# Second scan of a Mamba-like layer: one pair of states from matmuls with diagonals of B back to GpSimd, and three or four pairs times C there

## The chip, the cores and the metric

The kernel runs on one core of one Trainium2 chip. It is one launch, and the metric is the device time of that launch in microseconds (us). Engines are named TensorE (PE; its weight loads PEld), VectorE (DVE), ScalarE (ACT), GpSimd (POOL) and SyncE (SP, whose queue issues most DMAs).

## The reference, cut to what matters

A gated layer of two halves. The first is a selective state-space layer over four sequences of 1024 positions with 1024 channels and 16 states; the second is a feed-forward block with attention for 128 chosen rows of each sequence. The part touched here is the scan of the first half:

```python
delta = jax.nn.softplus(jnp.einsum('er,brl->bel', dt_proj_w, dt_lo) + dt_proj_b[None, :, None])
A = -jnp.exp(A_log)

def step(state, xs):
    d_t, B_t, C_t, u_t = xs
    dA = jnp.exp(d_t[..., None] * A)
    state = state * dA + (d_t * u_t)[..., None] * B_t[:, None, :]
    y_t = jnp.einsum('ben,bn->be', state, C_t)
    return (state, y_t)
...
y = y + D[None, :, None] * u
y = y * jax.nn.silu(z)
```

## The kernel before

**Stages.** `project_stage` (the first two sequences), `scan_stage` with `first` = 0, `choose_and_attend`, `scan_stage` with `first` = 2 (the second scan, sequences 2 and 3), `choose_and_attend` again with what is left of the feed-forward block. Each stage begins when the one ahead of it is done on all engines. The second scan carries feed-forward matmuls of the first two sequences beside it (`fill`); the first scan carries projections of the last two (`early`).

**Units and chunks.** A scan is 32 units, each one tile of 128 channels by 512 positions. Eight units (all 1024 channels) are a chunk; a sequence has two chunks, so a scan has chunks 0 to 3. In chunks 1 and 3 (called odd; `s // NE % H2` is 1) the scans start from a carry that the chunk ahead left. The 16 states of a unit are handled as 8 pairs, 0 to 7.

**One pair.** ScalarE makes dA = exp(delta A) of its two states. delta u B, the added term, comes from one of three places: GpSimd's product (`quad`, the most common, a whole instruction for the states of a group of four that are its own), matmuls with diagonals of B on TensorE (pairs in `SCALED`), or TensorE's transposes of a term that ScalarE scaled in transposed form (pairs in `TURNED`). In the first case dA goes to the PSUM tile `pA` and the term lies in `x`; in the other two the term goes to `pA` and dA to `x`. `pA` has room for two pairs, the even and the odd ones taking turns, so a pair begins when the one two ahead is out of the way. VectorE scans each state (one instruction of 128x512). Then comes the product with C: on GpSimd for the pairs in `pool_pairs` (the scan then writes to `hp` in SBUF, three buffers), on VectorE for the others (the scan writes in place in `pA`). Both write to `x`. `add_pair` sums the pair into `py` with 8 transposing matmuls; after all eight pairs `gate` on VectorE multiplies by the gate, and GpSimd adds the input (`add_x`).

**What sets the order.** Each engine has one queue, written out by hand in loops over units and pairs, and waits on semaphores in it. On GpSimd a unit s runs: product with C of pair 7 of unit s-1; `quad(s, 2)`, `quad(s, 3)`; C of pair 1; a feed-forward merge in some units; `begin(s + 1)`, which makes the next delta and delta u; C of pair 3; `add_x(s - 1)`; `quad(s + 1, 0)`; C of pair 5; `quad(s + 1, 1)`; C of pair 6. On TensorE: `make_b(1)`, sum of pair 5 of the unit ahead, sum of 6, `make_b(3)`, sum of 7, gate and skip transposes, sum of 0, `make_b(5)`, sum of 1, transposes of the next delta u, sums of 2 and 3, `make_b(7)`, sum of 4, with feed-forward matmuls (`beside`) in between. `make_b(i)` waits for pair i-2: for its product if VectorE makes that, for its scan if GpSimd does. `quad` waits until the sum of the unit ahead has read the part of `x` that it writes. On VectorE a unit is scan of the first state, product with C of the pair ahead (if it is VectorE's), scan of the second state, for pairs 0 to 7; `gate` of the unit ahead stands before pair 3, and two small feed-forward operations stand in some units.

Before the change both scans have `TURNED` = (3, 7) and `SCALED` = (1, 5). `make_diagonals` on GpSimd writes the diagonals of B once a chunk for each scaled pair, two selects each.

Of the kernel before, what the change touches and what calls it, by code (L numbers as in the profile page):

```python
# [25 lines left out]
NE = DI // P  # L26
# [5 lines left out]
H2 = L // HALF  # L32
# [6 lines left out]
SPAN = 2  # L39
# [35 lines left out]
        self.ropes = ctx.enter_context(nc.sbuf_tensor(f"c{first}_ropes", [P, SPAN, 2 * DH], F32))  # L75


TURNED, SCALED = (3, 7), {0: (1, 5), SPAN: (1, 5)}


def states_by_pool(first):
# [287 lines left out]


def pool_pairs(first, s):
    return (1, 3, 5, 6, 7) if s // NE % H2 else (1, 3, 5, 7)


def vec_pairs(first, s):
    return tuple(i for i in range(NPAIR) if i not in pool_pairs(first, s))
# [37 lines left out]
def scan_stage(nc, t, ctx, keep, first, late_taps=None):  # L414
# [14 lines left out]
    scaled = SCALED[first]  # L429
    from_pe = tuple(sorted(TURNED + scaled))  # L430
    NF, ND_B = 2 * len(from_pe), 2 * len(scaled)
    pool_order = [(s, i) for s in range(UNITS) for i in pool_pairs(first, s)]
    vec_order = [(s, i) for s in range(UNITS) for i in vec_pairs(first, s)]
    pool_count = {at: k + 1 for k, at in enumerate(pool_order)}
# [73 lines left out]
    def chunk(s):  # L508
        return s // NE
# [22 lines left out]
    def b_at(s, n):  # L532
        return NF * s + 2 * from_pe.index(n // 2) + n % 2 + 1

    def column(n):
        return 2 * (n // 4) + n % 2
# [15 lines left out]
    with nc.Block() as block:  # L552
# [161 lines left out]
        def _(pool):  # L714
            def begin(s):
                pool.wait_ge(soft_ready, s + 1)
                pool.tensor_tensor(out=delta[:, s % 2], in0=delta[:, s % 2], in1=du[:, s % 2], op=ALU.add).then_inc(delta_ready, 1)
                pool.wait_ge(delta_ready, s + 1)
                if s >= 2:
                    pool.wait_ge(u_in[s % 2], 16 * (s // 2))  # L720
                pool.tensor_tensor(out=du[:, s % 2], in0=delta[:, s % 2], in1=u[:, s % 2], op=ALU.mult).then_inc(du_ready, 1)

            def quad(s, g):
                if s >= UNITS:
                    return
                if g == 0:
                    pool.wait_ge(du_ready, s + 1)
                if s and s % NE == 0:
                    pool.wait_ge(B_in[g], 16 * chunk(s))
                into, n = quad_place(first, g)  # L730
                if s:
                    pool.wait_ge(summed, after_sum(s - 1, (4 * g + n - 1) // 2))
                pool.tensor_tensor(out=x[:, 4 * g:4 * g + n], in0=du[:, s % 2:s % 2 + 1].broadcast_to([P, n, HALF]),  # L733
                                   in1=bB[:, into:into + n], op=ALU.mult).then_inc(w_ready, 1)
# [6 lines left out]
            def make_diagonals(c, i):  # L741
                for n in (2 * i, 2 * i + 1):
                    k = 2 * scaled.index(i) + n % 2
                    if c:
                        pool.wait_ge(BT_in[c % 2], 16 * (NS // 2) * ((c + 1) // 2))
                        pool.wait_ge(b_ready, b_at(c * NE - 1, n))
                    pool.affine_select(out=diagB[:, k], in_=BT[:, c % 2, column(n)].rearrange("p (a o) -> p a o", o=1).broadcast_to([P, HALF // P, P]),
                                       compare_op=ALU.is_equal, fill=0.0, base=0, pattern=[[0, HALF // P], [-1, P]],
                                       channel_multiplier=1).then_inc(diag_ready, 1)

            def times_C(s, i):
                if i not in pool_pairs(first, s):
                    return
                pool.wait_ge(scanned, NS * s + 2 * i + 2)
                if s and s % NE == 0:
                    pool.wait_ge(C_in[i // 2], 16 * chunk(s))
                pool.tensor_tensor(out=x[:, 2 * i:2 * i + 2], in0=hp_of(s, i), in1=bC[:, 2 * i:2 * i + 2],  # L757
                                   op=ALU.mult).then_inc(pool_hc, 1)
# [3 lines left out]
            def add_x(s):  # L762
                pool.wait_ge(y_used, s + 1)
                pool.wait_ge(xt_in[s % 3], ring3(s)[1])
                pool.tensor_tensor(out=xt[:, s % 3], in0=xt[:, s % 3], in1=gy[:, s % 3], op=ALU.add).then_inc(x2_ready, 1)

            def merge(begin, end):
                for p in range(NI // 2):
                    if begin <= up_slot[p] + MERGE_LAG < end:
                        pool.wait_ge(swish_ready, p + 1)  # L770
                        pool.wait_ge(up_ready, p + 1)
                        both = hidden[:, 2 * p:2 * p + 2].rearrange("p m r -> p (m r)")
                        pool.tensor_tensor(out=both, in0=both, in1=swish[:], op=ALU.mult).then_inc(hidden_ready, 1)

            def root(begin, end):
                if begin <= POW_AT < end:
                    pool.wait_ge(mean_ready, 1)
                    pool.wait_ge(exponent, 1)
                    pool.tensor_tensor(out=squares[:], in0=squares[:], in1=minus_half[:], op=ALU.pow).then_inc(pow_ready, 1)
# [8 lines left out]
            for s in range(UNITS):  # L788
                last_tile = s % NE == NE - 1 and s + 1 < UNITS
                if s:  # L790
                    times_C(s - 1, 7)
                quad(s, 2)
                quad(s, 3)
                times_C(s, 1)
                if fill:
                    merge(NPAIR * s, NPAIR * s + NPAIR // 2)
                if s + 1 < UNITS:
                    begin(s + 1)
                if last_tile and scaled:
                    make_diagonals(chunk(s) + 1, scaled[0])  # L800
                if fill:
                    root(NPAIR * s, NPAIR * s + NPAIR // 2)
                times_C(s, 3)
                if s:
                    add_x(s - 1)
                quad(s + 1, 0)
                times_C(s, 5)
                if last_tile and scaled:
                    make_diagonals(chunk(s) + 1, scaled[1])
                quad(s + 1, 1)  # L810
                if fill:
                    merge(NPAIR * s + NPAIR // 2, NPAIR * (s + 1))
                    root(NPAIR * s + NPAIR // 2, NPAIR * (s + 1))
                times_C(s, 6)
# [1582 lines left out]
```

## Time and profile before

| | us |
|---|---|
| median of 3 runs | 2808.98 |
| lowest and highest | 2807.94, 2814.0 |
| profiled execution, its own time | 2810.57 |
| its span | 2808.7 |
| second scan, first scan instruction to last gate, by the trace | 1248.0 to 2110.6 |

The span is the time from the first to the last record of the one profiled execution; its own time holds the launch as well. Busy times of an engine are sums over that span. PE's shares need care: matmuls are pipelined, a diagonal matmul is recorded twice, and the printed duration of one is longer than the distance to the next. Where an engine's cadence is meant, starts are compared.

### The profile page before, as it was taken

What the parts mean: (1) busy time and instruction counts of PE and PEld (TensorE: products, weight loads), DVE (VectorE), ACT (ScalarE), POOL (GpSimd) and SP (SyncE); (2) the same over time, 40 slices, a digit from 0 to 9 for tenths busy, and PEclk for the clock granted to TensorE, in tenths of its full rate; (3) what the DMA queues carried; (4) which work ended last, traced back from release to release, by engine and by line L of the source; (5) the groups of instructions that cost most, each with busy time, mean ns of one, the idle gap of its engine ahead of it and who ended that gap; (6) DMA issues with size and microseconds to landing.
All of it is one profiled execution on the core that took longest, in us unless ns stands there. A gap on an engine that the chain in (4) does not pass through costs nothing. (4 is left out here: it accounts for less than half of the span.)

```text
span 2808.7 us, 38267 instructions
## 1 busy us (share of the span) xinstructions
PE 2534.9 (90%) x13528; PEld 1853.5 (66%) x13528; DVE 1964.8 (70%) x2500; ACT 1616.4 (58%) x3482; POOL 1616.2 (58%) x898
## 2 busy tenths in 40 slices
PE   8979999989999657879999999999997799999998
PEld 3356666666666426556688988888673576578853
DVE  5679999989999786569998988999896544110000
ACT  4578888778887442277787787887661215210000
POOL 1269999999999610028899998889881100000000
PEclk9979999999999858999999999999998899999999
DMA  7732242442332397863344344244228741344442
GB/s 277 260 87 83 64 144 80 127 115 64 116 92 80 110 405 263 291 192 99 121 135 129 103 153 146 84 167 146 85 76 311 273 151 38 97 158 150 152 155 97
DMA packets 252622, 412.53 MB, mean 147 GB/s; under 512 B 50832, under 2 KB 134800, under 8 KB 249872
## 3 DMA queue, kind: packets, MB, share of 16 engines
q1 hardware_dynamic: 238928, 353.98, 39.4%
q10 hardware_dynamic: 12160, 51.39, 4.6%
q0 software_dynamic: 1344, 4.72, 0.5%
q8 instruction: 108, 1.77, 0.3%
q14 instruction: 82, 0.67, 0.1%
HBM read 325.09 MB, written 84.94 MB: 146 GB/s over the span
## 5 line engine op out<-in xcount | busy, mean ns | idle before, releaser
L757 POOL TENSOR_TENSOR s_x<-s_hp,k_bC 128x1024 f32<-128x1024 f32 x288 | 680.2, 2368 | 68.2 <-DVE s_hp L1290 67.7
L733 POOL TENSOR_TENSOR s_x<-s_du,k_bB 128x1024 f32<-128x1024 f32 x254 | 601.5, 2377 | 39.2 <-PE s_py L882 23.6
L882 PE MATMUL s_py<-k_ident,s_x 128*128 128x128 f32 x4096 | 522.2, 274 | 21.4 <-POOL s_x L757 21.4
L882 PEld LDWEIGHTS s_py<-k_ident,s_x 128*128 128x128 f32 x4096 | 463.8, 142 | 32.6 <-POOL s_x L757 28.5
L1214 ACT ACTIVATE s_pA<-s_delta,k_negA 128x512 f32<-128x512 f32 x512 | 333.6, 681 | 190.6 <-DVE s_x L1267 185.1
L1983 PE MATMUL l_p<-l_hT,l_ring 128*128 128x256 f32 x1792 | 389.4, 380 | 2.0 <-ACT l_hT L2088 1.0
L1983 PEld LDWEIGHTS l_p<-l_hT,l_ring 128*128 128x128 f32 x1792 | 341.6, 191 | 49.6 <-issue 1.5
L1290 DVE TENSOR_TENSOR_SCAN s_hp<-s_x,s_carry,s_pA 128x512 f32<-128x512 f32 x256 | 321.7, 1267 | 44.5 <-PE s_pA L864 36.1
L1214 ACT ACTIVATE s_x<-s_delta,k_negA 128x512 f32<-128x512 f32 x512 | 340.6, 710 | 0.0
L1290 DVE TENSOR_TENSOR_SCAN s_hp<-s_x,s_pA 128x512 f32<-128x512 f32 x256 | 310.0, 1211 | 42.3 <-ACT s_x L1214 26.5
L1092 ACT ACTIVATE s_xT<-s_duT,k_BT 128x128 f32<-128x128 f32 x1024 | 336.4, 389 | 0.1
L864 PEld LDWEIGHTS s_pA<-k_bB,s_duT 128*128 128x128 f32 x2048 | 251.0, 196 | 86.2 <-DVE s_hp L1290 68.0
L1290 DVE TENSOR_TENSOR_SCAN s_pA<-s_pA,s_x 128x512 f32<-128x512 f32 x256 | 299.8, 1214 | 4.4 <-ACT s_pA L1214 4.0
L864 PE MATMUL s_pA<-k_bB,s_duT 128*128 128x128 f32 x2048 | 262.8, 283 | 23.0 <-DVE s_hp L1290 23.0
L1267 DVE TENSOR_TENSOR s_x<-s_pA,k_bC 128x1024 f32<-128x1024 f32 x224 | 268.7, 1199 | 17.7 <-DMA k_bC<-scratch_xd 17.7
L1290 DVE TENSOR_TENSOR_SCAN s_pA<-s_pA,s_carry,s_x 128x512 f32<-128x512 f32 x192 | 234.6, 1268 | 1.0 <-ACT s_pA L1214 0.8
L1960 POOL DMA_INDIRECT out_dram<-c_rows,l_row_i x2 | 1.9, 953 | 330.8 <-DVE c_rows L2309 330.8
L862 PEld LDWEIGHTS s_pA<-k_ident,s_xT 128*128 128x128 f32 x1024 | 116.5, 142 | 97.4 <-DVE s_hp L1290 72.1
L862 PE MATMUL s_pA<-k_ident,s_xT 128*128 128x128 f32 x1024 | 135.9, 276 | 39.1 <-DVE s_hp L1290 39.1
L2304 DVE TENSOR_TENSOR t_hidden<-l_silu,l_p 128x256 f32<-128x256 f32 x32 | 13.5, 421 | 208.0 <-PE l_p L1983 208.0
L1990 PE MATMUL l_p<-l_ring,t_hidden 128*128 128x512 f32 x352 | 151.4, 592 | 0.0
L1950 POOL TENSOR_TENSOR l_squares<-l_squares,l_minus_half 128x1 f32<-128x1 f32 x2 | 1.1, 555 | 250.3 <-DVE l_squares L2280 250.3
(238 smaller groups left out, 3770.4 us busy)
## 6 DMA issues: line engine op xcount, KB each, us to landing
k_bC<-scratch_xd SPq DMA_DIRECT2D x32, 1024.0 KB, 11.0
scratch_ug<-p_ug ACTq DMA_DIRECT2D x16, 1024.0 KB, 4.1
k_u<-scratch_ug SPq DMA_DIRECT2D x64, 256.0 KB, 3.5
k_bB<-scratch_xd SPq DMA_DIRECT2D x32, 512.0 KB, 8.3
s_gy<-scratch_ug SPq DMA_DIRECT2D x64, 256.0 KB, 4.5
s_xt<-in_x SPq DMA_DIRECT2D x64, 256.0 KB, 4.8
scratch_x<-s_xt SPq DMA_DIRECT2D x64, 256.0 KB, 3.6
r_x<-scratch_x SPq DMA_DIRECT2D x32, 512.0 KB, 10.2
```

The lines of the kernel that those rows point to most:

```text
L733: pool.tensor_tensor(out=x[:, 4 * g:4 * g + n], in0=du[:, s % 2:s % 2 + 1].broadcast_to([P, n, HALF]), in1=bB[:, into:into + n], op=ALU.mu ...
L757: pool.tensor_tensor(out=x[:, 2 * i:2 * i + 2], in0=hp_of(s, i), in1=bC[:, 2 * i:2 * i + 2], op=ALU.mult).then_inc(pool_hc, 1)
L862: last = nc.tensor.transpose(out, xT[:, k, a * P:(a + 1) * P], ident[:])
L864: last = nc.tensor.matmul(out, duT[:, a * P:(a + 1) * P], diagB[:, 2 * scaled.index(i) + n % 2, a], start=True, stop=True)
L882: last = nc.tensor.matmul(py[:, a], x[:, n, a * P:(a + 1) * P], ident[:], is_transpose=True, start=False, stop=n == NS - 1 and a == HALF / ...
L1092: last = nc.scalar.activation(xT[:, k, a * P:(a + 1) * P], duT[:, a * P:(a + 1) * P], ACT.Copy, scale=BT[:, chunk(s) % 2, column(2 * TURNE ...
L1214: nc.scalar.activation(out, delta[:, s % 2], ACT.Exp, scale=negA[:, s % NE, n:n + 1]).then_inc(dA_ready, 1)
L1267: nc.vector.tensor_tensor(x[:, 2 * i:2 * i + 2], pA[:, j:j + 2], bC[:, 2 * i:2 * i + 2], ALU.mult).then_inc(vec_hc, 1)
L1290: nc.vector.tensor_tensor_scan(out, dA, added, initial, ALU.mult, ALU.add).then_inc(scanned, 1)
L1983: last = nc.tensor.matmul(out[:, 0:ROWS], w[:, c * P:(c + 1) * P], src[:, c], start=c == 0, stop=c == KT - 1)
L1990: last = nc.tensor.matmul(banks[2 * a + h][:], src[:, a * P:(a + 1) * P], w[:, h * HALF:(h + 1) * HALF], start=is_first, stop=is_last)
L2304: nc.vector.tensor_tensor(hidden[:, m], silu[:, m % 2], acc[2 + m % 2][:, 0:ROWS], ALU.mult).then_inc(act_ready, 1)
```

## The change

`SCALED` of the second scan is (5,) instead of (1, 5). So pair 1's term is GpSimd's again: `states_by_pool` has ten states instead of eight, and the first group of four is whole, which makes `quad(s, 0)` one instruction of 128x2048 where it was 128x1024. Pair 1's dA goes to `pA` instead of `x`. `make_b(s, 1)` and pair 1's diagonals are gone. `quad(s + 1, 0)` now waits for the sum of pair 1 where it waited for that of pair 0. `pool_pairs` of the second scan's odd chunks is (1, 5, 7) instead of (1, 3, 5, 6, 7); the even chunks keep (1, 3, 5, 7). So VectorE multiplies pairs 3 and 6 by C in the odd chunks. The first scan stays as it was.

```diff
-TURNED, SCALED = (3, 7), {0: (1, 5), SPAN: (1, 5)}
+TURNED, SCALED = (3, 7), {0: (1, 5), SPAN: (5,)}
...
 def pool_pairs(first, s):
+    if first:
+        return (1, 5, 7) if s // NE % H2 else (1, 3, 5, 7)
     return (1, 3, 5, 6, 7) if s // NE % H2 else (1, 3, 5, 7)
...
-                if last_tile and scaled:
-                    make_diagonals(chunk(s) + 1, scaled[0])
+                if last_tile and 1 in scaled:
+                    make_diagonals(chunk(s) + 1, 1)
...
-                if last_tile and scaled:
-                    make_diagonals(chunk(s) + 1, scaled[1])
+                if last_tile and 5 in scaled:
+                    make_diagonals(chunk(s) + 1, 5)
```

GpSimd, second scan, a unit of chunk 0, from the delta of the next unit on (L717, L721: delta and delta u; L757: product with C; L765: the input; L733: product with B). Before:

```order
L717 TENSOR_TENSOR s_delta<-s_delta,s_du 128x512
L721 TENSOR_TENSOR s_du<-s_delta,k_u 128x512
L757 TENSOR_TENSOR s_x<-s_hp,k_bC 128x1024
L765 TENSOR_TENSOR s_xt<-s_xt,s_gy 128x512
L733 TENSOR_TENSOR s_x<-s_du,k_bB 128x1024
L757 TENSOR_TENSOR s_x<-s_hp,k_bC 128x1024
L733 TENSOR_TENSOR s_x<-s_du,k_bB 128x1024
L757 TENSOR_TENSOR s_x<-s_hp,k_bC 128x1024
L733 TENSOR_TENSOR s_x<-s_du,k_bB 128x1024 x2
L757 TENSOR_TENSOR s_x<-s_hp,k_bC 128x1024
```

The same place now (lines are two further down in the changed file):

```order
L719 TENSOR_TENSOR s_delta<-s_delta,s_du 128x512
L723 TENSOR_TENSOR s_du<-s_delta,k_u 128x512
L759 TENSOR_TENSOR s_x<-s_hp,k_bC 128x1024
L767 TENSOR_TENSOR s_xt<-s_xt,s_gy 128x512
L735 TENSOR_TENSOR s_x<-s_du,k_bB 128x2048
L759 TENSOR_TENSOR s_x<-s_hp,k_bC 128x1024
L735 TENSOR_TENSOR s_x<-s_du,k_bB 128x1024
L759 TENSOR_TENSOR s_x<-s_hp,k_bC 128x1024
L735 TENSOR_TENSOR s_x<-s_du,k_bB 128x1024 x2
L759 TENSOR_TENSOR s_x<-s_hp,k_bC 128x1024
```

Nothing moved; the first product with B is twice as wide. The same stretch of a unit of chunk 1 (with the merge, L773) before:

```order
L717 TENSOR_TENSOR s_delta<-s_delta,s_du 128x512
L721 TENSOR_TENSOR s_du<-s_delta,k_u 128x512
L757 TENSOR_TENSOR s_x<-s_hp,k_bC 128x1024
L765 TENSOR_TENSOR s_xt<-s_xt,s_gy 128x512
L733 TENSOR_TENSOR s_x<-s_du,k_bB 128x1024
L757 TENSOR_TENSOR s_x<-s_hp,k_bC 128x1024
L733 TENSOR_TENSOR s_x<-s_du,k_bB 128x1024
L773 TENSOR_TENSOR t_hidden<-t_hidden,s_swish 128x512
L757 TENSOR_TENSOR s_x<-s_hp,k_bC 128x1024 x2
L733 TENSOR_TENSOR s_x<-s_du,k_bB 128x1024 x2
L757 TENSOR_TENSOR s_x<-s_hp,k_bC 128x1024
```

and now:

```order
L719 TENSOR_TENSOR s_delta<-s_delta,s_du 128x512
L723 TENSOR_TENSOR s_du<-s_delta,k_u 128x512
L767 TENSOR_TENSOR s_xt<-s_xt,s_gy 128x512
L735 TENSOR_TENSOR s_x<-s_du,k_bB 128x2048
L759 TENSOR_TENSOR s_x<-s_hp,k_bC 128x1024
L735 TENSOR_TENSOR s_x<-s_du,k_bB 128x1024
L775 TENSOR_TENSOR t_hidden<-t_hidden,s_swish 128x512
L759 TENSOR_TENSOR s_x<-s_hp,k_bC 128x1024
L735 TENSOR_TENSOR s_x<-s_du,k_bB 128x1024 x2
L759 TENSOR_TENSOR s_x<-s_hp,k_bC 128x1024
```

The products with C of pairs 3 (ahead of L765) and 6 (one of the two behind the merge) are gone. VectorE, a unit of chunk 1, from gate on (the scans are printed as SCALAR_TENSOR_TENSOR at L1290; L1267 is the product with C), before:

```order
L1256 TENSOR_TENSOR s_gy<-s_py,s_gy 128x512
L1290 SCALAR_TENSOR_TENSOR s_hp<-s_x,s_carry,s_pA 128x512
L1267 TENSOR_TENSOR s_x<-s_pA,k_bC 128x1024
L1290 SCALAR_TENSOR_TENSOR s_hp<-s_x,s_carry,s_pA 128x512
L1290 SCALAR_TENSOR_TENSOR s_pA<-s_pA,s_carry,s_x 128x512 x2
L1290 SCALAR_TENSOR_TENSOR s_hp<-s_x,s_carry,s_pA 128x512
L1267 TENSOR_TENSOR s_x<-s_pA,k_bC 128x1024
```

and now:

```order
L1258 TENSOR_TENSOR s_gy<-s_py,s_gy 128x512
L1292 SCALAR_TENSOR_TENSOR s_pA<-s_x,s_carry,s_pA 128x512
L1269 TENSOR_TENSOR s_x<-s_pA,k_bC 128x1024
L1292 SCALAR_TENSOR_TENSOR s_pA<-s_x,s_carry,s_pA 128x512
L1292 SCALAR_TENSOR_TENSOR s_pA<-s_pA,s_carry,s_x 128x512
L1269 TENSOR_TENSOR s_x<-s_pA,k_bC 128x1024
L1292 SCALAR_TENSOR_TENSOR s_pA<-s_pA,s_carry,s_x 128x512
L1292 SCALAR_TENSOR_TENSOR s_hp<-s_x,s_carry,s_pA 128x512
L1269 TENSOR_TENSOR s_x<-s_pA,k_bC 128x1024
```

Pair 3's scans write to `pA`, and its product with C stands between the two scans of pair 4.

## Rows read from the trace of the kernel before

**Rows 1.** The page: busy time and share of each engine.

```profile
PE 2534.9 (90%) x13528; PEld 1853.5 (66%) x13528; DVE 1964.8 (70%) x2500; ACT 1616.4 (58%) x3482; POOL 1616.2 (58%) x898
```

**Rows 2.** GpSimd's delta addition, second scan: ns min/median/max, first and last start.

```profile
L717 POOL TENSOR_TENSOR s_delta<-s_delta,s_du x31: 1260/1277/1328, 1259.7 to 2067.0; 128x512 f32<-128x512 f32 x31
```

**Rows 3.** Windows: length; busy PE, PEld, DVE, ACT, POOL; clock, DMA, GB/s.

```profile
221.62:344.48 122.86, 112.72 (x712) 81.59 (x711) 116.37 (x106) 105.80 (x256) 112.34 (x55) 1.00 0.26 74
421.76:520.64 98.88, 91.42 (x571) 66.02 (x570) 91.98 (x81) 79.25 (x169) 98.57 (x49) 1.00 0.25 75
1286.11:1389.63 103.52, 100.33 (x598) 71.65 (x596) 96.48 (x90) 79.17 (x188) 89.89 (x46) 1.00 0.32 102
1526.49:1631.84 105.35, 104.01 (x709) 92.95 (x708) 95.78 (x88) 82.99 (x172) 102.59 (x52) 1.00 0.33 106
1743.93:1848.79 104.86, 103.48 (x704) 92.40 (x703) 96.28 (x90) 87.31 (x203) 93.59 (x49) 1.00 0.33 106
1988.21:2066.97 78.76, 78.76 (x458) 55.52 (x457) 69.33 (x61) 56.00 (x117) 74.18 (x38) 1.00 0.39 120
```

**Rows 4.** Waits of VectorE in the second scan: us in total, times, longest.

```profile
DVE s_hp L1290 <- PE s_pA L864: 31.8, 15, 7.4
DVE s_gy L1256 <- PE s_py L882: 21.5, 24, 3.6
```

**Rows 5.** Timeline, unit of chunk 1: start, us, engine, line, [idle before <- releaser].

```profile
1570.79 1.95 PE L864 MATMUL s_pA<-k_bB,s_duT 128*128 128x128 f32 x16
1571.98 1.28 DVE L1290 TENSOR_TENSOR_SCAN s_hp<-s_x,s_carry,s_pA 128x512 f32<-128x512 f32 x1 [1.16 <-PE s_pA L864]
1572.58 1.04 PE L882 MATMUL s_py<-k_ident,s_x 128*128 128x128 f32 x8
1573.18 1.20 DVE L1267 TENSOR_TENSOR s_x<-s_pA,k_bC 128x1024 f32<-128x1024 f32 x1
1574.30 1.27 DVE L1290 TENSOR_TENSOR_SCAN s_hp<-s_x,s_carry,s_pA 128x512 f32<-128x512 f32 x1
```

**Rows 6.** Timeline of GpSimd, chunk 0: two products with B, then one with C.

```profile
1331.08 4.70 POOL L733 TENSOR_TENSOR s_x<-s_du,k_bB 128x1024 f32<-128x1024 f32 x2
1335.72 2.38 POOL L757 TENSOR_TENSOR s_x<-s_hp,k_bC 128x1024 f32<-128x1024 f32 x1
```

**Rows 7.** Groups by line, 1310 to 2100 us: busy us, mean ns of one.

```profile
L733 POOL TENSOR_TENSOR s_x<-s_du,k_bB 128x1024 f32<-128x1024 f32 x116 | 274.4, 2371 | 26.8 <-PE s_py L882 19.3 <-issue 7.3
...
L747 POOL TENSOR_SCALAR_AFFINE_SELECT k_bB<-k_BT 128x512 f32<-128x512 f32 x12 | 7.4, 640 | 0.0
```

**Rows 8.** Timeline of TensorE, chunk 1: pair 5's diagonal matmuls, pair 7's transposes.

```profile
1556.90 1.95 PE L864 MATMUL s_pA<-k_bB,s_duT 128*128 128x128 f32 x16
...
1564.78 1.04 PE L862 MATMUL s_pA<-k_ident,s_xT 128*128 128x128 f32 x8
```

**Rows 9.** Timeline, the three late places: VectorE's scans of pair 1, TensorE's wait.

```profile
1491.60 1.28 DVE L1290 TENSOR_TENSOR_SCAN s_hp<-s_x,s_carry,s_pA 128x512 f32<-128x512 f32 x1 [4.69 <-PE s_pA L864]
...
1676.39 1.22 DVE L1290 TENSOR_TENSOR_SCAN s_hp<-s_x,s_pA 128x512 f32<-128x512 f32 x1 [1.78 <-PE s_pA L864]
...
1972.60 1.60 PE L937 MATMUL s_p_gate<-s_ring,t_hidden 128*128 128x512 f32 x2 [4.10 <-POOL t_hidden L773]
...
1980.98 1.28 DVE L1290 TENSOR_TENSOR_SCAN s_hp<-s_x,s_carry,s_pA 128x512 f32<-128x512 f32 x1 [7.37 <-PE s_pA L864]
```

**Rows 10.** Timeline, unit 0: ScalarE's exponentials of pair 1, VectorE's scan of it.

```profile
1251.53 1.32 ACT L1214 ACTIVATE s_x<-s_delta,k_negA 128x512 f32<-128x512 f32 x2
...
1252.77 1.22 DVE L1290 TENSOR_TENSOR_SCAN s_hp<-s_x,s_pA 128x512 f32<-128x512 f32 x1 [2.40 <-PE s_pA L864]
```

**Rows 11.** Timeline of VectorE, first unit of chunk 1: product with C.

```profile
1476.33 1.22 DVE L1267 TENSOR_TENSOR s_x<-s_pA,k_bC 128x1024 f32<-128x1024 f32 x1 [2.81 <-DMA k_bC<-scratch_xd]
```

**Rows 12.** Timeline of TensorE, last unit: the sum of pair 7.

```profile
2108.78 1.10 PE L882 MATMUL s_py<-k_ident,s_x 128*128 128x128 f32 x8 [1.25 <-POOL s_x L757]
```

**Rows 13.** VectorE's products with C, 1290 to 2110 us: ns min/median/max, starts.

```profile
L1267 DVE TENSOR_TENSOR s_x<-s_pA,k_bC x106: 1195/1198/1225, 1292.4 to 2099.2; 128x1024 f32<-128x1024 f32 x106
```

## The prediction

> **What bounds the kernel now.** The page's first line comes first [rows 1]: TensorE 90%, VectorE 70%, ScalarE and GpSimd 58%. These are averages over stages with different limits, and the change touches one stage, the second scan. Its cadence is read from GpSimd's addition in begin(), issued once a unit [rows 2]: 31 of them from 1259.7 to 2067.0, so 807.3 / 30 = 26.9 us a unit. The reader should see that this stage costs some 860 us of 2808.7 and that all that follows starts after it, so whatever it gains or loses moves the end by as much.
>
> Next the windows [rows 3]. Each begins and ends at such an addition; they hold 5, 4, 4, 4, 4 and 3 undisturbed units: first scan, even and odd chunk, then chunks 0 to 3 of the second scan. Divided by those numbers:
> - chunk 0: 25.9 us a unit, TensorE busy 25.1, VectorE 24.1, GpSimd 22.5
> - chunk 1: 26.3; TensorE 26.0, VectorE 23.9, GpSimd 25.6
> - chunk 2: 26.2; TensorE 25.9, VectorE 24.1, GpSimd 23.4
> - chunk 3: 26.25; TensorE 26.25, VectorE 23.1, GpSimd 24.7
>
> TensorE is the bound (97% to 100% busy), and GpSimd is close behind in the odd chunks. The first scan has the same split of pairs but no feed-forward beside it: 24.7 us a unit in the odd chunk, with GpSimd at 98.57 of 98.88, so GpSimd can run with no gap at all; and 24.6 in the even one with VectorE busy 23.3, so VectorE keeps some 1.3 us of idle even where TensorE has room.
>
> The waits [rows 4] name what TensorE's load does: VectorE waited 31.8 us, 15 times, for diagonal matmuls and 21.5 us, 24 times, for the last sum ahead of gate(). In an odd unit [rows 5] TensorE gets to pair 1's matmuls at 1570.79, and VectorE, done before that, stands 1.16 us for them.
>
> **The change, part by part.** It is costed by the distance from start to start, not by the printed durations.
>
> TensorE: pair 1's 8 diagonal matmuls (16 records) leave every unit. They start at 1570.79, the next group at 1572.58 [rows 5]: 1.8 us a unit. TensorE falls to 23.3, 24.2, 24.1 and 24.4 us in chunks 0 to 3, well under the period.
>
> GpSimd: pair 1's product with B joins pair 0's in one instruction of 128x2048. Two of 128x1024 take 1331.08 to 1335.72, 2.32 each [rows 6]. No row has the wide form. A 128x512 operation takes 1.28 [rows 2], so from 512 to 1024 elements 1.04 is added, and two such steps, 2.1, are the lower end for the extra half; at most it costs 2.37, the mean of one [rows 7]. I take 2.3, since the spacing row is of the same operation. Even units keep four products with C, so GpSimd goes to 24.8 in chunk 0 and 25.7 in chunk 2. Odd units lose two of five: 2.3 - 2 x 2.32 = -2.3, so 23.3 and 22.4. Of the diagonals' selects, two of 0.64 us a chunk go [rows 7]; that is under the precision of the sum, and I count nothing.
>
> VectorE: only odd units change, by two products with C (pairs 3 and 6). One goes from 1573.18 to 1574.30 [rows 5], so +2.2 us: 26.2 in chunk 1, 25.3 in chunk 3. The scans keep their number, and whether one writes hp or pA makes no difference worth counting. ScalarE writes pair 1's two exponentials into pA instead of x; they must wait until pair 7's scans are done. Two scans lie between, 2.3 us, enough for two exponentials; where feed-forward work stands ahead of them on ScalarE it may cost one more of them, 0.7 us (its 1.32 for two, [rows 10]). Bounds 0 and 0.7, and I take 0, since VectorE's wait for pair 1 goes at the same place.
>
> The Trainium skill, Perfetto Trace Analysis, section GPSIMD Engine Instruction, says that GpSimd's spans don't compose and to use the spacing from start to start. The trace agrees: 2.37 printed, 2.32 apart. By printed spans GpSimd's even units would come out 0.05 us a product longer, which changes nothing below.
>
> Now the new periods: the busiest engine, and what idle time stays.
> - Chunk 0: the floor is GpSimd's 24.8, and VectorE's 24.1 plus the 1.3 of idle seen in the first scan is 25.4. I take 25.3, -0.6 a unit, x 8 = -4.8.
> - Chunk 2: GpSimd 25.7 with little gap, 25.9 against 26.2: -0.3, x 8 = -2.4.
> - Chunk 1: VectorE 26.2 is now the floor. One new wait comes with it: TensorE's matmuls for pair 5 write where pair 3 lay, and so they now wait for VectorE's product of pair 3, not for its scan. Behind that wait on TensorE stand the sum of pair 1, feed-forward matmuls and, 7.9 us on (1556.90 to 1564.78, [rows 8]), pair 7's transposes, for which VectorE waits in turn. From the end of that product VectorE has about 7.7 us of work up to pair 7 and TensorE 8.5 until its first half is there: 0.6 us of idle. I take 26.8 against 26.3: +0.5, x 8 = +4.0.
> - Chunk 3: VectorE 25.3, the same wait with less to do beside it, 1.0 us of idle: 26.35 against 26.25: +0.1, x 8 = +0.8.
>
> Single places, outside the windows:
> - Three times TensorE is late by itself and pair 1's matmuls stand between it and VectorE [rows 9]: after a late weight tile (VectorE idle 4.69), at the turn to chunk 2 (1.78), and where the down projection waits for GpSimd's last merge (7.37). With those matmuls gone VectorE runs on through pairs 1 and 2, but then waits for pair 3's transposes behind the same work; only the 1.8 us come back: 3 x -1.8 = -5.4.
> - Start [rows 10]: VectorE stands 2.40 us for pair 1's first matmuls, until 1252.77. The wait won't go whole: ScalarE begins pair 1's exponentials only at 1251.53, so the scan could begin at 1252.3: -0.4.
> - At the turns to chunks 1 and 3 VectorE stands 2.81 us [rows 11] (and about the same again) for C's second half; there pair 3's added product runs inside that wait: 2 x -1.1 = -2.2.
> - Last unit [rows 12]: TensorE waits for GpSimd's product of pair 7, whose scan VectorE now ends one product later: +1.1.
>
> Sum: -4.8 + 4.0 - 2.4 + 0.8 - 5.4 - 0.4 - 2.2 + 1.1 = -9.3 us, of which the single places are -6.9. The profiled execution took 2810.6 us, its span 2808.7, the median of the runs is 2809.0; the sum goes from the median: **2800 us**.
>
> **Rivals.**
> 1. Give and take cancel. The gains come from several engines that each stand a per cent or two under the period, and they don't add. If the even units gain only 0.2 us and the odd ones cost 0.6 (the new wait costs more, ScalarE's later exponentials are felt), it is 16 x -0.2 + 16 x 0.6 - 6.9 = -0.5, so 2808.5. For it: in chunk 2 GpSimd's 25.7 is already close to 26.2. Against: the single places don't depend on it.
> 2. Slower: VectorE becomes the bound of the odd units and keeps its idle. In chunk 1 it idles 26.3 - 23.9 = 2.4 us a unit today; if the wait at pair 5 holds TensorE so that every later handover is as late as now, the two products add in full, 16 x 2.2 = +36, less what else is won (-4.8 - 2.4 - 6.9 = -14): +22, 2831. It decides from 0.6 us more idle in each odd unit than I take (9.3 / 16). For it: TensorE stands in order, so each wait for VectorE delays work that VectorE needs later. Against: [rows 5] shows that today's idle comes from TensorE's load, 1.8 us of which goes, and in the first scan's even chunk four of VectorE's products a unit go with 1.3 us of idle.
> 3. VectorE's and GpSimd's products hinder each other. Against: VectorE's 106 products took 1195 to 1225 ns [rows 13] although GpSimd was busy through nearly all of them. Were each of the 32 added ones held up by one of GpSimd's, it would be 32 x 2.3 = +74 on top of the -9: 2874. The Trainium skill, Perfetto Trace Analysis, section Optimizing Scalar/DVE Operations, warns that the two share a read port and that moving work between them might not help; the row speaks against it here. That the change doesn't do what it says is next to excluded: the order of the instructions shows it.
>
> The Trainium skill, GPSIMD Engine Reference, section Engine selection, would have elementwise products on VectorE, as GpSimd is about two times slower. The rows agree (2.32 against 1.12). Half of this change follows it, half goes against it, and by the rule alone it would be a gain in the odd units; there the periods above say a small loss, because it is the fuller engine that counts.
>
> **How the numbers follow.** Forecast 0.54, with a range of its own from 2787 to 2803; rival 1 0.25; rival 2 0.18; rival 3 or nothing 0.03. The range for eight in ten starts below the forecast's own, where chunk 2 and the odd units do as well as chunk 0 (-0.6 and 0 a unit: -4.8 - 4.8 - 6.9 = -16.5) and the unshown rest of the turns between chunks gives half of what the three late places do, another 8: 2784. Up it takes in rival 1 and two thirds of the way from there to rival 2: 2824. 0.2% is 5.6 us, about what a measurement can tell. Faster than 2803.4: 0.54. Within: 0.24, nearly all of it rival 1. Slower than 2814.6: 0.22, rivals 2 and 3 and the upper end of 1.
>
> **What would show it.** Right: in chunks 0 and 2 GpSimd busy over 98% and a period of 25.3 and 25.9; in chunks 1 and 3 VectorE busy over 96%, TensorE under 93%, periods of 26.8 and 26.35; no wait of VectorE for pair 1; TensorE waiting for VectorE's products ahead of pair 5's matmuls. Wrong: a period over 27.5 in chunk 1, or GpSimd in chunks 0 and 2 with gaps while the period stays at 26.

## The result, and the profile after

| | us |
|---|---|
| before, median of 4 runs (lowest, highest) | 2808.46 (2806.68, 2814.0) |
| changed, median of 4 runs (lowest, highest) | 2831.61 (2827.38, 2834.3) |
| ratio | 1.0078, interval 1.0058 to 1.0097 |
| changed, span of the profiled execution | 2825.3 |

The changed kernel is slower by 23 us, where 9 us faster was forecast. The time is outside the range (2784 to 2824) and within a microsecond of rival 2's price (2831). The profiled execution was the fastest of its four (2827.38), so its span shows 17 us of the loss.

The page's first line, beside [rows 1]: TensorE and GpSimd have less to do, VectorE has more, as the change says.

```profile
PE 2491.1 (88%) x13016; PEld 1795.7 (64%) x13016; DVE 2002.9 (71%) x2532; ACT 1619.4 (57%) x3482; POOL 1603.9 (57%) x859
```

The windows, made as in [rows 3], of 4, 4, 4 and 3 units of chunks 0, 1, 2 and 3 (length; busy PE, PEld, DVE, ACT, POOL; granted clock, DMA share, GB/s):

```profile
1283.36:1383.60 100.24, 93.36 (x534) 64.30 (x533) 96.72 (x91) 79.77 (x190) 98.18 (x46) 1.00 0.33 106
1521.50:1630.60 109.10, 97.94 (x638) 84.29 (x637) 104.92 (x95) 83.46 (x171) 92.52 (x44) 1.00 0.32 102
1744.20:1848.93 104.73, 99.56 (x653) 86.31 (x652) 97.84 (x91) 87.28 (x203) 101.83 (x48) 1.00 0.33 106
1996.30:2080.74 84.44, 77.68 (x412) 53.64 (x411) 77.42 (x68) 56.89 (x117) 66.55 (x31) 0.96 0.36 113
```

| us a unit | before | forecast | changed |
|---|---|---|---|
| chunk 0 | 25.9 | 25.3 | 25.1 |
| chunk 1 | 26.3 | 26.8 | 27.3 |
| chunk 2 | 26.2 | 25.9 | 26.2 |
| chunk 3 | 26.25 | 26.35 | 28.1 |

Whole chunks, from one unit's delta addition to that of eight units later (six in chunk 3), took 210.0, 219.4, 216.8 and 161.1 us before, and 208.6, 223.2, 215.8 and 173.8 now; from the last addition to the last gate it was 42.9 and is 48.4. So the loss lies in the odd chunks, most of it in chunk 3 and the end.

What stands there is one chain, here in a unit of chunk 1 (timeline: start, us, engine, line; in brackets the idle time ahead and what ended it):

```profile
1552.80 1.21 DVE L1269 TENSOR_TENSOR s_x<-s_pA,k_bC 128x1024 f32<-128x1024 f32 x1
1554.06 2.05 PE L866 MATMUL s_pA<-k_bB,s_duT 128*128 128x128 f32 x16 [2.60 <-DVE s_x L1269]
1555.36 1.28 DVE L1292 TENSOR_TENSOR_SCAN s_hp<-s_x,s_carry,s_pA 128x512 f32<-128x512 f32 x1 [0.15 <-PE s_pA L866]
1557.13 4.56 POOL L735 TENSOR_TENSOR s_x<-s_du,k_bB 128x2048 f32<-128x2048 f32 x1 [3.73 <-PE s_py L884]
1561.60 1.04 PE L864 MATMUL s_pA<-k_ident,s_xT 128*128 128x128 f32 x8
1562.34 1.28 DVE L1292 TENSOR_TENSOR_SCAN s_hp<-s_x,s_carry,s_pA 128x512 f32<-128x512 f32 x1 [0.21 <-PE s_pA L864]
```

VectorE's product of pair 3 (1552.80) releases TensorE's matmuls for pair 5, for which TensorE has stood 2.60 us. Behind them is the sum of pair 1, and for that GpSimd's wide product stands 3.73 us. Over the second scan (waits: total, times, longest):

```profile
POOL s_x L735 <- PE s_py L884: 70.2, 16, 7.1
PE s_pA L866 <- DVE s_x L1269: 34.9, 16, 4.1
DVE s_hp L1292 <- PE s_pA L864: 17.3, 20, 2.2
POOL s_x L735 <- DMA k_bB<-scratch_xd: 12.3, 2, 7.1
DVE s_x L1269 <- DMA k_bC<-scratch_xd: 7.5, 3, 2.8
PE s_p_gate L939 <- POOL t_hidden L775: 6.4, 1, 6.4
```

Sixteen times, once in each odd unit, TensorE waits for pair 3's product. VectorE's wait for pair 1's diagonals, part of the first line of [rows 4], is gone, as was meant.

### The profile page after: what moved, and what is told of

The parts are those of the page before. It is cut to its first block and busy times, and to the rows that moved or that the text cites. A ratio compares the mean times of both kernels' runs of the same rounds, so it can differ in the third digit from the quotient of the medians.

```text
span 2825.3 us, 37151 instructions
## 1 busy us (share of the span) xinstructions
PE 2491.1 (88%) x13016; PEld 1795.7 (64%) x13016; DVE 2002.9 (71%) x2532; ACT 1619.4 (57%) x3482; POOL 1603.9 (57%) x859
## 5 line engine op out<-in xcount | busy, mean ns | idle before, releaser
L735 POOL TENSOR_TENSOR s_x<-s_du,k_bB 128x1024 f32<-128x1024 f32 x254 | 666.7, 2637 | 91.9 <-PE s_py L884 71.1
L759 POOL TENSOR_TENSOR s_x<-s_hp,k_bC 128x1024 f32<-128x1024 f32 x256 | 605.3, 2368 | 42.9 <-DVE s_hp L1292 42.7
L884 PE MATMUL s_py<-k_ident,s_x 128*128 128x128 f32 x4096 | 525.3, 275 | 25.9 <-POOL s_x L759 24.4
L1216 ACT ACTIVATE s_pA<-s_delta,k_negA 128x512 f32<-128x512 f32 x576 | 375.3, 681 | 197.7 <-DVE s_x L1269 192.2
L1269 DVE TENSOR_TENSOR s_x<-s_pA,k_bC 128x1024 f32<-128x1024 f32 x256 | 307.3, 1200 | 16.3 <-DMA k_bC<-scratch_xd 16.3
L1216 ACT ACTIVATE s_x<-s_delta,k_negA 128x512 f32<-128x512 f32 x448 | 298.0, 710 | 15.7 <-DVE s_x L1269 15.7
L1292 DVE TENSOR_TENSOR_SCAN s_hp<-s_x,s_pA 128x512 f32<-128x512 f32 x224 | 271.1, 1210 | 27.5 <-ACT s_x L1216 18.0
L1292 DVE TENSOR_TENSOR_SCAN s_pA<-s_pA,s_carry,s_x 128x512 f32<-128x512 f32 x224 | 275.6, 1269 | 5.0 <-ACT s_pA L1216 4.4
L1292 DVE TENSOR_TENSOR_SCAN s_hp<-s_x,s_carry,s_pA 128x512 f32<-128x512 f32 x192 | 242.3, 1269 | 35.1 <-PE s_pA L866 16.7
L866 PEld LDWEIGHTS s_pA<-k_bB,s_duT 128*128 128x128 f32 x1536 | 190.0, 200 | 113.9 <-DVE s_hp L1292 60.7
L866 PE MATMUL s_pA<-k_bB,s_duT 128*128 128x128 f32 x1536 | 203.7, 288 | 55.2 <-DVE s_x L1269 34.9
```

The costliest lines, as they stand in the source:

```text
L866: last = nc.tensor.matmul(out, duT[:, a * P:(a + 1) * P], diagB[:, 2 * scaled.index(i) + n % 2, a], start=True, stop=True)
L884: last = nc.tensor.matmul(py[:, a], x[:, n, a * P:(a + 1) * P], ident[:], is_transpose=True, start=False, stop=n == NS - 1 and a == HALF / ...
L1216: nc.scalar.activation(out, delta[:, s % 2], ACT.Exp, scale=negA[:, s % NE, n:n + 1]).then_inc(dA_ready, 1)
L1269: nc.vector.tensor_tensor(x[:, 2 * i:2 * i + 2], pA[:, j:j + 2], bC[:, 2 * i:2 * i + 2], ALU.mult).then_inc(vec_hc, 1)
L1292: nc.vector.tensor_tensor_scan(out, dA, added, initial, ALU.mult, ALU.add).then_inc(scanned, 1)
```

## The experiments

Two explanations were set against each other. **Handover**: what counts is which engine makes pair 3's product with C. While it is GpSimd's, TensorE's matmuls for pair 5 wait for pair 3's scan; once it is VectorE's, they wait for the product, which comes a scan and a product later. **Load**: each product that VectorE gets more in an odd unit, where it has 26.2 us of work in a period of 26.3, costs its own time, wherever it stands. All kernels below are the changed one with the edit that is shown, if nothing else is said. Each ratio is to the kernel before, run beside it; its medians there were 2809.0 to 2810.3.

### Which pairs, at the same load

```diff
-        return (1, 5, 7) if s // NE % H2 else (1, 3, 5, 7)
+        return (1, 3, 5, 7)
```

> The changed kernel, but in the second scan's odd chunks GpSimd multiplies pairs 1, 3, 5, 7 by C (four, as in the even ones), so VectorE gets one product more than before the change (pair 6) and not pair 3's. Handover theory (pair 3's product on VectorE holds TensorE ahead of pair 5's matmuls, and behind that GpSimd's product with B): TensorE's wait for VectorE's product at pair 5 is gone in all 16 odd units, GpSimd is the fullest engine of all units, odd units take 25.9 us in chunk 1 and 25.3 in chunk 3 instead of 27.3 and 27.3 to 28.3; the time is 2785 to 2800, below both kernels. Load theory (each product that VectorE gets more in an odd unit costs its own 1.1 us): half of the loss goes, 2818 to 2822.

Measured 2796.05 us (ratio to before 0.9952, 0.9936 to 0.9969). The second kernel has (1, 5, 6, 7) in the odd chunks, so the same number of products on each engine, but pair 3's on VectorE:

> The changed kernel, but in the second scan's odd chunks GpSimd multiplies pairs 1, 5, 6, 7 by C: the same numbers of products on each engine as with 1, 3, 5, 7, but it is pair 3's that VectorE makes. Handover theory: TensorE still waits some 2 us for that product in each odd unit, and the time stays within 6 us of the changed kernel, 2824 to 2836. Load theory: as with 1, 3, 5, 7, 2818 to 2822.

Measured 2831.19 us (1.0073, 1.0056 to 1.009). Load would have had both at 2820. The 35 us between them are the price of the handover at equal load, 2.2 us a unit in the mean of the 16 odd ones. The changed kernel has one product more on VectorE than the second (pair 6's) and takes the same time, so that product costs nothing beside it. In the first, windows of 4 units of chunk 1 and 3 of chunk 3 read

```profile
1522.33:1624.91 102.58, 97.49 (x639) 84.65 (x638) 100.02 (x91) 83.42 (x172) 101.81 (x49) 1.00 0.34 109
1979.66:2054.71 75.05, 75.05 (x417) 50.88 (x416) 74.41 (x66) 56.34 (x117) 73.53 (x35) 1.00 0.40 127
```

that is 25.6 and 25.0 us a unit (25.9 and 25.3 were expected) with three engines 95% to 99% busy in the first window. In the second, TensorE waits for the product as in the changed kernel:

```profile
PE s_pA L866 <- DVE s_x L1269: 33.0, 16, 3.5
```

### The wait made shorter, work unchanged

VectorE's product of pair 3 moved ahead of pair 4's first scan:

```diff
+                    ahead = fill and i == 4 and 3 not in pool_pairs(first, s)
+                    if ahead:
+                        times_C(s, 3)
                     scan(s, 2 * i)
-                    times_C(s, i - 1)
+                    if not ahead:
+                        times_C(s, i - 1)
```

> The changed kernel with VectorE's product of pair 3 ahead of pair 4's first scan instead of behind it, so that TensorE gets its release one scan (1.2 us) sooner; each engine's work is unchanged. Handover theory: TensorE's wait for that product falls by about 1 us in each odd unit, from 35 us to under 20, and the time by 12 to 20: 2811 to 2820. Load theory: no change, 2826 to 2835. Against it: VectorE's scans of pair 4 come one product later, which delays ScalarE's exponentials for pair 6.

Measured 2810.98 us (1.0009, 0.9999 to 1.0019), 21 less than the changed kernel, with TensorE's wait down from 34.9 us to 18.1:

```profile
PE s_pA L866 <- DVE s_x L1269: 18.1, 15, 2.9
```

Next, the sum of pair 1 put ahead of pair 5's matmuls, which fills the wait with work:

```diff
+                if fill:
+                    add_pair(s, 1)
                 if 5 in from_pe:
                     make_b(s, 5)
-                add_pair(s, 1)
+                if not fill:
+                    add_pair(s, 1)
```

> The changed kernel with the sum of pair 1 ahead of pair 5's matmuls on TensorE in the second scan, so that it no longer stands behind their wait. GpSimd's wait for the sum falls from some 4 us in an odd unit to under 1.5. It fills 0.9 us of TensorE's wait with work in odd units, and delays pair 5's matmuls by 0.9 us in even ones. Handover theory: odd units gain up to 0.9 us each for pair 7 (16 x 0.5 = 8), even ones lose nothing or 0.3: 2820 to 2830. Load theory: no change, 2828 to 2834.

Measured 2810.46 us (0.9998, 0.9989 to 1.0008): again 21 us, below the 2820 to 2830 expected. TensorE's wait fell to 19.1 us. Both gained more than TensorE's wait for the product lost (16 to 17 us).

### GpSimd's wait behind it

GpSimd's wait for the sum (70 us) is the longest in the list. The wide product was cut in two, pair 1's half behind the product with C of pair 5:

```diff
+            def second_pair(s):
...
+                pool.wait_ge(summed, after_sum(s - 1, 1))
+                pool.tensor_tensor(out=x[:, 2:4], in0=du[:, s % 2:s % 2 + 1].broadcast_to([P, 2, HALF]),
+                                   in1=bB[:, 2:4], op=ALU.mult).then_inc(w_ready, 1)
...
+                second_pair(s + 1)
```

> The changed kernel with GpSimd's 128x2048 product with B cut in two of 128x1024: pair 0's where the wide one stood, waiting only for the sum of pair 0, pair 1's behind the product with C of pair 5, waiting for the sum of pair 1. If GpSimd's wait for the sum of pair 1 (70 us in all) is what makes the odd units long, it vanishes and the time falls by 8 to 20 us, to 2811 to 2823, and TensorE's wait for the last merge falls from 6.4 us. If only the wait of TensorE for VectorE's product counts, the time stays at 2826 to 2834, since GpSimd has 4 us of room in an odd unit.

Measured 2832.61 us (1.0082, 1.0065 to 1.0099), no gain. GpSimd's wait for the sum fell from 70.2 to 8.9 us, and TensorE's for the last merge from 6.4 to 4.9. GpSimd's idle time went to another wait, for VectorE's scans:

```profile
POOL s_x L770 <- DVE s_hp L1304: 85.9, 27, 9.9
...
PE s_pA L878 <- DVE s_x L1281: 32.9, 16, 4.1
```

So the longest wait of the list is not what makes the odd units long: GpSimd has room there (23.1 us of 27.3 in chunk 1), and taking it out only let GpSimd stand elsewhere.

### Each part of the change alone

Pair 1's term on GpSimd alone, with (1, 3, 5, 6, 7) times C in the odd chunks:

> One part of the change alone: pair 1's term goes from diagonal matmuls to GpSimd in the second scan, while the pairs times C there stay 1, 3, 5, 7 and 1, 3, 5, 6, 7. VectorE's work is that of before. Handover theory: TensorE waits for no product of pair 3; GpSimd has ten products in an odd unit and is the bound, 28.0 us in chunk 1 and 27.1 in chunk 3 against 26.3 and 26.25: 8 x 1.7 + 8 x 0.9, less 4 for the even chunks, +17: 2824 to 2832, with GpSimd busy over 98% in the odd chunks. Load theory gives the same here, since it is GpSimd's load; the run prices this part.

Measured 2825.49 us (1.0069, 1.0052 to 1.0085). GpSimd is the bound there, 28.1 us a unit (window of 3 units of chunk 1):

```profile
1522.57:1606.88 84.31, 77.52 (x486) 66.97 (x487) 71.62 (x66) 61.68 (x130) 84.08 (x40) 0.96 0.32 100
```

The pairs times C alone, with pairs 1 and 5 on the diagonals: 

> The other part alone: pairs 1 and 5 stay on the diagonal matmuls in both scans, and in the second scan's odd chunks GpSimd multiplies 1, 5, 7 by C instead of 1, 3, 5, 6, 7. Handover theory: TensorE is as full as before the change (26.0 to 26.3 us a unit) and now also stands 2 us in each odd unit for VectorE's product of pair 3, so these add: odd units 28 to 29 us, 2835 to 2850, slower than the changed kernel. Load theory: VectorE's 26.2 us stay below TensorE's 26.3, so the time is that of before or up to 10 more, 2808 to 2820.

Measured 2847.06 us (1.0137, 1.0121 to 1.0154). And in that same place (1, 3, 5, 7), so that pair 3 stays on GpSimd:

> The kernel before (pairs 1 and 5 on diagonal matmuls) with pairs 1, 3, 5, 7 times C in the second scan's odd chunks: VectorE gets pair 6's product more, pair 3's stays on GpSimd. Against the run with 1, 5, 7 in the same place (2847 us) it tells the price of pair 3's handover where TensorE is full. Handover theory: one product more on VectorE (25.0 us of 26.3) costs nothing: 2804 to 2812. Load theory: half of the 38 us of that run, 2826 to 2830.

Measured 2811.3 us (1.0005, 0.9995 to 1.0015). One product more on VectorE (pair 6's) costs nothing that can be measured. Pair 3's on top of it costs 36 us, with TensorE full; here the loads aren't equal, since VectorE has that product more and GpSimd has it less. The parts alone lose 16 and 38 us, together 23. Each eases the engine that the other fills: with 1, 5, 7 times C GpSimd has 23.1 us a unit of chunk 1 instead of 28, and without pair 1's diagonals TensorE is 90% busy there. How much of the difference is due to which was not tried.

### The turns between chunks

Chunk 0 gained 1.3 us as a whole, where its four undisturbed units gained 3.3. At a turn GpSimd, with less work ahead in its queue, now stands longer ahead of its first product with B, until B has landed. The changed kernel, turn to chunk 2:

```profile
1662.71 1.22 SPq L603 DMA_DIRECT2D k_bB<-scratch_xd  x2
...
1670.36 4.55 POOL L735 TENSOR_TENSOR s_x<-s_du,k_bB 128x2048 f32<-128x2048 f32 x1 [7.08 <-DMA k_bB<-scratch_xd]
```

B is issued at 1662.71, just before GpSimd is there (1663.28), because that DMA stands behind the load of u on SyncE, which waits for TensorE's skip of the unit. Moved ahead of it, in the kernel with (1, 3, 5, 7):

```diff
+                if fill and e == NE - 1:
+                    load_B(c, 0)
+                if fill and e == 0 and s:
+                    load_C(c - 1, 2)
+                    load_C(c - 1, 3)
                 load_u(s + 2)
...
-                if e == 0 and s:
+                if not fill and e == 0 and s:
                     load_C(c - 1, 2)
                     load_C(c - 1, 3)
...
-                    load_B(c, 0)
+                    if not fill:
+                        load_B(c, 0)
```

> The kernel with pairs 1, 3, 5, 7 in the odd chunks too (2796 us), with two of the loads at the turns between chunks issued sooner in the second scan: B's first quarter and C's last two quarters stand ahead of the load of u on SyncE, which waits for TensorE's skip of that unit. If the waits at the turns (GpSimd for B 14 us in 3, VectorE for C 10 us in 3) lie on the path, the turns shorten by 2 to 5 us each: 2783 to 2791. If they are hidden by the rest of the turn, 2794 to 2797. The length of the loads can grow where they collide with the weight tiles.

Measured 2775.13 us (0.9881, 0.9864 to 0.9897), 34 us below the one before and below the 2783 to 2791 expected; the last kernel below can't be told from it, and all others are slower. GpSimd passes the same turn with no wait for B:

```profile
1647.05 2.36 POOL L765 TENSOR_TENSOR s_x<-s_hp,k_bC 128x1024 f32<-128x1024 f32 x1 [0.22 <-DVE s_hp L1298]
1650.59 4.55 POOL L741 TENSOR_TENSOR s_x<-s_du,k_bB 128x2048 f32<-128x2048 f32 x1
```

The same loads moved in the kernel before and in the changed one:

> The kernel before with the loads at the turns issued sooner, as in the 2775 us kernel. In its trace GpSimd waits for B at the turns too (7.3 us in 3) and VectorE for C (9.6 us in 3). If the early loads gain what the waits are worth whatever the split of pairs, 2790 to 2797; if TensorE, which is full there, holds the turns anyway, 2800 to 2806.

> The changed kernel with the loads at the turns issued sooner. Tells how much of its miss lies at the turns and how much in the handover of pair 3: if the turns cost the changed kernel as much as the one with pairs 1, 3, 5, 7, it falls by some 20 us to 2807 to 2814, and what stays above 2775 (32 to 39 us) is the handover. If the turns are hidden behind the handover, 2820 to 2830.

Measured 2793.56 (0.9941, 0.9924 to 0.9958) and 2817.62 us (1.0029, 1.0019 to 1.0039). So the turns are worth 16 us in the kernel before, 14 in the changed one and 21 in the one with (1, 3, 5, 7). GpSimd's wait for B is gone in all three. The changed kernel's time lies between the two ranges that were expected. With the turns out of the way the change still costs 24 us (2817.6 against 2793.6), so they aren't why it is slower.

Last, the sum of pair 1 moved ahead in the 2775 us kernel, where pair 5's matmuls wait for no product:

> The 2775 us kernel (pairs 1, 3, 5, 7, early loads) with the sum of pair 1 ahead of pair 5's matmuls. TensorE waits there only for a scan, and GpSimd's product with B waits for no sum, so the handover theory says nothing is left to win: 2772 to 2779. If the order of TensorE's queue gained the 21 us of the changed kernel by anything but that wait, this gains too: below 2770.

Measured 2774.87 us (0.9879, 0.9861 to 0.9897): nothing. So the 21 us that this move gained in the changed kernel came from the wait.

## Why the prediction was wrong

**The step that failed** is the price of the new wait in the terms of chunks 1 and 3. The prediction named the chain (pair 3's product, pair 5's matmuls, 7.9 us later pair 7's transposes), and its lengths were right: 1554.06 to 1561.60 is 7.5 us, VectorE's load in chunk 1 is 104.92 / 4 = 26.2 us. But it priced the wait only by VectorE's idle time in one undisturbed unit, 0.6 and 1.0 us, 12.8 us in all, and set that against what TensorE gains, so that the odd chunks were to cost +4.8 us. Measured at equal load the wait costs 35 us, 2.2 us a unit. What the sum left out:
- In chunk 1 VectorE idles 27.3 - 26.2 = 1.0 us a unit. Its waits for TensorE at pairs 5 and 7 are 2.5 us in the four units, so 0.6 a unit, as forecast; the other 0.4 are short waits (for ScalarE among others) that the sum put at nothing. The clock was 1.00.
- In chunk 3 it idles 28.15 - 25.8 = 2.3 us, and TensorE's clock falls. Two units of the changed kernel, one after the other:

```profile
2025.60:2052.39 26.79, 24.54 (x138) 16.67 (x136) 25.53 (x23) 18.96 (x39) 22.21 (x11) 1.00 0.32 99
2052.39:2080.74 28.35, 26.10 (x137) 18.27 (x136) 25.49 (x23) 18.96 (x39) 22.18 (x11) 0.94 0.46 149
```

  The first is 0.4 us above the 26.35 forecast. The second is 1.6 us longer with the same work. It holds pair 5's matmuls at half speed, 3.66 us instead of 2.05, right behind a wait of 2.25 (granted clock 0.53 from 2057.66 to 2061.30). The same wait stood ahead of them in the first unit:

```profile
2030.90 2.05 PE L866 MATMUL s_pA<-k_bB,s_duT 128*128 128x128 f32 x16 [2.25 <-DVE s_x L1269]
...
2057.66 3.66 PE L866 MATMUL s_pA<-k_bB,s_duT 128*128 128x128 f32 x16 [2.25 <-DVE s_x L1269]
```

  What the clock costs there can be read from the changed kernel with the early loads, of which the last stand in the turn to chunk 3, some 100 us earlier. The same three units of chunk 3 have the same waits (6.8 us in 3) and the same work, but the clock stayed at 1.00, and they took 81.2 us instead of 84.4:

```profile
1985.87:2067.05 81.18, 74.43 (x412) 50.40 (x411) 77.41 (x68) 56.87 (x117) 66.50 (x31) 1.00 0.37 117
```

  So the slow clock is a part of the price and not the whole. At a clock of 1.00 and equal load, the last unit in the window of chunk 3 with pair 3's product on VectorE, (1, 5, 6, 7), still takes 2.15 us more than with it on GpSimd, (1, 3, 5, 7):

```profile
2061.24:2087.99 26.75, 24.50 (x137) 16.67 (x136) 24.23 (x22) 18.85 (x40) 24.51 (x13) 1.00 0.51 157
...
2030.11:2054.71 24.60, 24.60 (x140) 16.80 (x139) 24.39 (x23) 18.78 (x39) 24.52 (x13) 1.00 0.53 171
```

- Around the unit where the down projection waits for GpSimd's last merge, 1.8 us were to come back. The merge stood behind the product with B that waits for the sum of pair 1, and TensorE's wait there grew from 4.10 us [rows 9] to 6.41. With (1, 3, 5, 7) it grew as well, to 7.1; with the sum ahead of pair 5's matmuls it was 4.1 again. But that unit and the one ahead of it together took 57.7 us before, 57.7 with (1, 3, 5, 7), and 66.0 in the changed kernel, where TensorE stood 4.09 us for pair 3's product, longer than in any undisturbed unit, and pair 5's 16 records behind it took 3.78 us. How these 8 us divide was not tried.

Sorted by the marks of the whole chunks in the profiled executions (chunk 3 with the end), the forecast was -4.8, -0.7, -2.4 and -1.0 us, and -1.3, +3.8, -1.0 and +18.1 were measured: two thirds of the error lie in chunk 3 and the end. The working also has two slips: 8.5 - 7.7 is 0.8 us of idle, not 0.6 (1.6 us over chunk 1), and rival 2's 16 x 2.2 is 35, not 36.

**GpSimd and the even units: right but for chunk 2.** The wide product takes 4.55 us against 4.64 for two, the low side of the bounds. Chunk 0 fell to 25.1 us a unit (25.3 forecast) with GpSimd 98% busy. Chunk 2 came out at 26.2, not 25.9, with GpSimd busy 25.5 of it, one of the signs that the prediction named for being wrong: the small term of -2.4 wasn't in its undisturbed units. What holds them was not tried.

**Places outside the windows: too hopeful.** The start gained 0.5 us, as forecast (0.4): VectorE's scan of pair 1 began at 1252.31 instead of 1252.77. The three turns were to give back 5.8 us (the late weight tile, the turn to chunk 2, twice 1.1). GpSimd's wait for B grew from 7.3 us in the three turns to 15.8 (12.3 by the list above and one of 3.5; the trace names no releaser for that one and the 7.3, but all of them are gone with the early loads), and the last units of chunks 0, 1 and 2 took 30.5, 31.8 and 32.2 us where 28.8, 30.2 and 28.9 had been. The units right behind them took 25.0, 26.6 and 23.3 where 29.8, 28.5 and 24.7 had been, so the turns gained 1.5 us in all, and not 5.8. The prediction asked which stall goes there, not what is late next when GpSimd is early.

**Rivals.** Rival 1 (2808.5) had the odd units cost 0.6 us each; they cost 1.0 in chunk 1 and 1.9 in chunk 3. Rival 2 gave the mechanism, TensorE held in order at pair 5, and 2831 us, the measured time. Its condition, 0.6 us more idle in each odd unit than the forecast took, was the right one to weigh (0.4 in chunk 1 and 1.3 in chunk 3); it got 0.18. But its price had both products add in full, 2.2 us in every odd unit. The undisturbed ones grew by 1.0 and 1.9, and the rest came from the two units at the last merge, the end, and turns that gave back less, so the sum was met partly by luck. Rival 3 is out: VectorE's products took 1201 ns in the mean, against a median of 1198 before [rows 13]:

```profile
L1269 DVE TENSOR_TENSOR s_x<-s_pA,k_bC 128x1024 f32<-128x1024 f32 x133 | 159.7, 1201 | 7.5 <-DMA k_bC<-scratch_xd 7.5
```

## What to carry to other kernels

When work moves from one engine to another, ask first what release it carries: here two splits with the same load on each engine differ by 35 us, because one lets TensorE start on a scan and the other only on a product behind it. Such a wait on a queue in order, met once in every iteration, should be priced over the whole loop, with the engine's clock, the places where the engine is late already, and all that stands behind, not by the gap that one undisturbed iteration shows. The longest wait of a list may cost nothing and the cure of a short one may pay: the sum moved ahead gained 21 us, the split that cut a wait of 70 us to 9 gained none, and a load moved out from behind an unrelated wait gained 14 to 21.

## What the runs showed of the hardware

TensorE's granted clock fell in some stretches of the second scan where it had waited some 2 us once a unit, and not in others. In chunk 3 it was 1.00 in the undisturbed windows with (1, 3, 5, 7) and of the kernel before, and 0.96 in the changed kernel over three units (77.68 us busy of 84.44), with the same 16 records at 2.05 us in one unit and 3.66 in another behind equal waits. Against it: with the early loads those three units had the same waits at 1.00, and the changed kernel's window of chunk 1 is at 1.00 with waits of up to 2.60 us. What decides it is open. The two edits that cut the wait to 1.2 and 1.4 us in those units ran them at 1.00. In the kernel with pair 1's term alone on GpSimd it was 0.96 in chunk 1 as well, at 92% busy. A GpSimd product of 128x2048 takes 4.55 us, against 2.36 for 128x1024.
